# An 11th table looked up by one-hots, Gram blocks transposed straight out of PSUM, and tables loaded through embT

## The chip, the cores and the metric

The kernel runs on one core of a Trainium2 chip. The metric is the device time of one execution in microseconds (us). The program is written for each engine by hand: TensorE (PE; its weight loads appear as PEld), VectorE (DVE), ScalarE (ACT), GpSimd (POOL) and SyncE (SP) each run their own list of instructions in order, and meet only at semaphores.

## What is computed

2048 samples are scored by a recommender tower. Each sample has 27 ids, one for each of 27 tables with rows of 128 floats; tables have 1000, 1250, 12500 or 125000 rows.

```
e = stack([tbl_0[ids[:, 0]], ..., tbl_26[ids[:, 26]]], axis=1)   # 2048 x 27 x 128
dot = einsum('bnd,bmd->bnm', e, e)                              # 27 x 27 for each sample
z = the 351 entries of dot below its diagonal
h = concatenate([z, dense_ctx], axis=1)                         # 2048 x 367
h = maximum(h @ W_top1 + b_top1, 0)                             # 512
h = maximum(h @ W_top2 + b_top2, 0)                             # 256
y = h @ W_top3                                                  # 2048 x 1
```

## The kernel before

**Staging.** The samples go in 8 pairs `p` of 2 tiles `t` of 128 samples. Pair 0 and pair 7 are written out apart (`first`, `last`), pairs 1 to 6 are a hardware loop. The embeddings of a tile are wanted transposed, in `embT`, with the 128 numbers of a row on the partitions and 27 slots for each sample.

**Two ways to fetch a row.** Ten tables of 1000 rows stand in SBUF (`parts`, each split into a high and a low half so that two fp32r products give the fp32 value). A row is picked by a product with a one-hot matrix: DVE compares the ids with the row numbers (8 instructions for a table, four buffers `onehot`), PE does 16 matmuls for a table and 256 samples (`lookup`, L641), ACT copies two tables at a time to `embT`. The other 17 tables are gathered: POOL issues one indirect DMA for each tile and table (L376), 34 in a pair, into `rows`. `rows` has one buffer for each tile, so the gathers for pair p+1 start when PE has transposed the first group of tile t of pair p (`transpose_rows`, five groups `TR` of 4, 4, 4, 3 and 2 tables), and run beside what PE does next. POOL keeps one gather queued ahead of the one that runs (`one_queued`).

**A pair on PE** is: 160 lookup matmuls (with the first layer of the pair before between them), then for each tile 17 transposes, some calls of the MLP of the pair before, and `gram`: 128 products of 27 slots with themselves (L672; an fp32 matmul has two rows in the trace, so 256 rows for a tile), in two halves into two PSUM tiles. DVE copies the first half, ACT the second, to `blocks` (`keep_blocks`, L543 and L444); DVE then transposes 32 x 32 blocks of it to `turned` (`turn`, L551) and picks the 351 entries into `z`. After the second tile come the third layer, the transposes of `z` of tile 0, and the lookups of the next pair.

**Pair 0.** The ten tables come in through four staging buffers, in `turned`, `h1` and `blocks`, so a table's load waits until the one four places before it has been split: ACT makes the high half (L398), DVE the low one (L519). ACT makes two of pair 0's one-hots (`ACT_ONEHOTS`). Pair 0 looks up eight tables; the rows of tables 8 and 9 are gathered (`early_rows`, 4 indirect DMAs, L386) and transposed. A one-hot buffer is free when PE is done with its last table (`slot_free`). SP issues, in this order, tables, ids, weights, `dense_ctx`, and the ids of pair 1 that the gathers need (`load_idx`, L282).

```
STAGES = 4
TR = [range(0, 4), range(4, 8), range(8, 12), range(12, 15), range(15, 17)]
CALLS_AFTER = [{2: 2, 4: 4}, {2: 3, 4: 5}]
...
for k in range(STAGES, NM):
    sp.wait_ge(s_high, k - STAGES + 1)
    sp.wait_ge(s_low, k - STAGES + 1)
    load_table(k)
```

Of the kernel before, what the change touches and what calls it, by code (L numbers as in the profile page):

```python
# [44 lines left out]
GATHERED = [f for f in range(NF) if f not in MM_TABLES]  # L45
NG = len(GATHERED)
SLOTS = GATHERED + MM_TABLES
PARTS = 2

STAGES = 4  # L50
OH = 4

# [4 lines left out]
TR = [range(0, 4), range(4, 8), range(8, 12), range(12, 15), range(15, 17)]  # L57
NT = len(TR)

EARLY = range(NM - LOOK_TABLES, NM)  # L60
BUILT = NM - len(EARLY) - len(ACT_ONEHOTS)


JOBS = LOOK + TILES * NT
EMB_BANKS = 4
BANK = [k % EMB_BANKS for k in range(JOBS)]
BY_DVE = LOOK * [0] + TILES * [0, 1, 0, 1, 0]
DVE_JOBS = sum(BY_DVE)
ACT_JOBS = JOBS - DVE_JOBS

IDS = [range(0, 2), range(2, OH), range(OH, NM)]


CALLS_AFTER = [{2: 2, 4: 4}, {2: 3, 4: 5}]
# [6 lines left out]
def row_job(t, k):  # L81
    return LOOK + t * NT + k
# [4 lines left out]
GS = 16  # L87
STEPS = G // GS
# [28 lines left out]
def dlrm_tower(nc, ids, ids_mm, ident_in, dense_ctx, tables, W1, b1, W2, b2, W3, out):  # L117
    with ExitStack() as ctx:
# [9 lines left out]
        def sb_view(tile, first, dims, start=0, count=P):  # L128
# [6 lines left out]
        row_of = sb("row_of", [P, CH], F32)  # L135
        row_of_i = sb("row_of_i", [P, CH], I32)
# [5 lines left out]
        parts = sb("parts", [P, NM, PARTS, CH * D], F32R)  # L142

        idx = sb("idx", [P, TILES, NF], I32)
        rows = sb("rows", [P, TILES, NG, D], F32)
        early_rows = sb("early_rows", [P, TILES, len(EARLY), D], F32)
        ids_b = sb("ids_b", [P, NM, W], I32)
        onehot = sb("onehot", [P, OH, CH, W], F32R)
        embT = sb("embT", [P, TILES, P * SLOT + COLS - NF], F32)
        blocks = sb("blocks", [P, TILES, NJ, G], F32)  # L150
        turned = sb("turned", [P, TILES, JEXT * 32], F32)
# [3 lines left out]
        h2 = sb("h2", [P, N2, W], F32)  # L155

        y = sb_view(early_rows, 0, [[1, W]], 0, 1)
        y_last = sb_view(early_rows, W, [[1, W]], 0, 1)
# [10 lines left out]
        s_early = sem("s_early")  # L169
        s_w1 = sem("s_w1")  # L170
        s_stage = [sem(f"s_stage{k}") for k in range(STAGES)]
# [22 lines left out]
        gram_dve = sem("gram_dve")  # L194
        gram_act = sem("gram_act")
# [27 lines left out]
        def looked(p, k):  # L223

            if isinstance(p, int) and p == 0:
                return k + 1
            return p * LOOK + k

        def slot_free(eng, p, f):

            if f % LOOK_TABLES:
                eng.wait_ge(emb_filled, p * JOBS + f // LOOK_TABLES + 1)
            else:
                eng.wait_ge(s_looked, looked(p, f // LOOK_TABLES))

        def lookup_views(k):

            pitch = P * SLOT + COLS - NF
            return (sb_view(embT, NG + LOOK_TABLES * k, [[1, LOOK_TABLES], [pitch, TILES], [SLOT, P]]),
                    emb_ps[BANK[k]][:].rearrange("d (f t b) -> d f t b", f=LOOK_TABLES, t=TILES))  # L240

# [13 lines left out]
        def block_views(t, s):  # L255

            src = gram_ps[s][:, 0:GS * NJ].rearrange("p (g j) -> p g j", g=GS)
            return sb_view(blocks, t * NJ * G + GS * s, [[1, GS], [G, NJ]]), src

# [3 lines left out]
        def _(sp):  # L263
# [7 lines left out]
            def ids_read(p, h):  # L271

                done = max(OH, IDS[h].stop)
                if isinstance(p, int) and p == 0:
                    done = min(done, EARLY.start)
                    sp.wait_ge(onehot_act, sum(f < done for f in ACT_ONEHOTS))
                    sp.wait_ge(s_onehot, done - sum(f < done for f in ACT_ONEHOTS))
                else:
                    sp.wait_ge(s_onehot, BUILT + (p - 1) * NM + done)
# [4 lines left out]
            def load_table(k):  # L284
                src = tables[MM_TABLES[k]].rearrange("(p c) d -> p (c d)", c=CH)
                load_in_two(sp, stage[k % STAGES], src, s_stage[k % STAGES])
# [13 lines left out]
            load_ids(0, 2)  # L300
            sp.dma_start(ident[:], ident_in).then_inc(s_ident, 16)
# [535 lines left out]
```

## Time and profile before

| What | Value |
|---|---|
| Time, median of 3 runs | 703.17 us (702.69 to 704.76) |
| Time of the profiled execution | 701.53 us |
| Its span, first to last instruction | 699.7 us |
| Busy: PE, PEld, DVE, ACT, POOL | 392.1, 344.1, 257.3, 157.7, 263.0 us |
| Mean granted TensorE clock | 0.741 of full speed |
| DMA | 35.77 MB, 51 GB/s |

Busy time is the time in which an engine has an instruction running. No engine is busy for much over half of the span. PE waits for nothing that the profile can name in much of its idle time: such time is called "issue".

### The profile page before, as it was taken

How to read it: one execution, taken by the hardware profiler on the slowest of the kernel's cores; microseconds unless marked ns; L12 is line 12 of the kernel's file. 1: busy time of each engine (PE TensorE's matmuls, PEld its weight loads, DVE VectorE, ACT ScalarE, POOL GpSimd, SP SyncE). 2: the span in 40 equal slices, each digit the busy share in tenths (PEclk: the TensorE clock that was granted, in tenths of full speed). 3: DMA queues.
4: the chain of work that ended last, by engine and by line, in shares of the span. 5: the costliest groups of instructions: out<-in, count | busy, mean ns of one | idle time of the engine just before them, and what ended most of it. 6: DMA issues, size and time to landing. Idle time of an engine off the chain costs nothing.

```text
span 699.7 us, 15045 instructions
## 1 busy us (share of the span) xinstructions
PE 392.1 (56%) x6064; PEld 344.1 (49%) x6064; DVE 257.3 (37%) x733; ACT 157.7 (23%) x212; POOL 263.0 (38%) x281
## 2 busy tenths in 40 slices
PE   3216332595437926297154954289361982559875
PEld 3116231593326915197143944179151971439754
DVE  5305122482134714085041921257140850417121
ACT  2407210032111402033020322014020330203321
POOL 6770547106371074503562064701645035630000
PEclk9657656597567966599575986679675895759998
DMA  8924311111121121111111211211111121110000
GB/s 202 232 53 122 94 31 50 47 50 41 24 53 44 48 53 28 45 32 65 45 38 28 75 38 30 53 39 50 49 34 41 32 65 45 38 27 2 2 2 1
DMA packets 22699, 35.77 MB, mean 51 GB/s; under 512 B 12921, under 2 KB 13569, under 8 KB 22674
## 3 DMA queue, kind: packets, MB, share of 16 engines
q0 software_dynamic: 8832, 18.11, 10.2%
q1 hardware_dynamic: 13842, 17.32, 9.0%
q8 instruction: 18, 0.29, 0.2%
q14 instruction: 7, 0.06, 0.0%
HBM read 35.39 MB, written 0.01 MB: 51 GB/s over the span
## 4 chain that ended last, share of the span: by engine, by line
PE 51%; issue 37%; another core or an unknown queue 4%; ACT 4%; DVE 2%; DMA 2%; SPq 1%; DVEq 0%; ACTq 0%
PE emb_ps L641 19%; PE gram_ps L672 14%; PE mlp_ps L691 5%; PE emb_ps L664 5%; PE mlp_ps L705 4%; DMA turned<-in_tbl 2%; PE mlp_ps L734 1%; PE mlp_ps L713 1%; DVE onehot L531 1%; PE mlp_ps L682 1%; ACT parts L398 1%; ACT embT L415 1%; PE mlp_ps L739 1%; SPq L253 1%
## 5 line engine op out<-in xcount | busy, mean ns | idle before, releaser
L376 POOL DMA_INDIRECT rows<-in_tbl,idx x272 | 258.9, 952 | 354.4 <-PE emb_ps L664 239.7
L672 PE MATMUL gram_ps<-embT 128*32 128x26 f32 x4096 | 99.5, 222 | 248.2 <-issue 244.6
L672 PEld LDWEIGHTS gram_ps<-embT 128*32 128x32 f32 x4096 | 78.2, 143 | 272.6 <-issue 269.7
L641 PE MATMUL emb_ps<-onehot,parts 125*128 125x256 f32 x1248 | 165.9, 292 | 47.3 <-issue 43.2
L531 DVE TENSOR_SCALAR onehot<-ids_b,row_of 128x256 fp32r<-128x256 int32 x608 | 167.3, 355 | 50.3 <-remote 29.2
L641 PEld LDWEIGHTS emb_ps<-onehot,parts 125*128 125x128 f32 x1248 | 159.7, 198 | 50.2 <-issue 44.7
L543 DVE COPY blocks<-gram_ps 128x416 f32<-128x416 f32 x16 | 14.6, 910 | 293.6 <-PE gram_ps L672 293.6
L444 ACT ACTIVATE blocks<-gram_ps 128x416 f32<-128x416 f32 x16 | 14.2, 885 | 333.5 <-PE gram_ps L672 333.5
L415 ACT ACTIVATE embT<-emb_ps 128x512 f32<-128x512 f32 x40 | 48.1, 1224 | 102.5 <-PE emb_ps L641 102.5
L537 DVE COPY embT<-emb_ps 128x512 f32<-128x512 f32 (+1 forms) x32 | 33.3, 1046 | 58.3 <-PE emb_ps L664 54.4
L419 ACT ACTIVATE embT<-emb_ps 128x512 f32<-128x512 f32 (+1 forms) x48 | 45.8, 1067 | 10.0 <-PE emb_ps L664 7.0
L664 PE MATMUL emb_ps<-ident,rows 128*128 128x128 f32 x272 | 41.8, 300 | 0.9 <-ACT embT L419 0.5
L691 PE MATMUL mlp_ps<-zT,w_sb 128*128 128x256 f32 (+1 forms) x168 | 39.8, 379 | 0.0
L664 PEld LDWEIGHTS emb_ps<-ident,rows 128*128 128x128 f32 x272 | 34.8, 155 | 4.7 <-ACT embT L419 1.0
L691 PEld LDWEIGHTS mlp_ps<-zT,w_sb 128*128 128x128 f32 (+1 forms) x168 | 30.2, 189 | 3.5
L705 PE MATMUL mlp_ps<-h,w_sb 128*128 128x256 f32 x112 | 28.7, 404 | 0.0
L705 PEld LDWEIGHTS mlp_ps<-h,w_sb 128*128 128x128 f32 x112 | 22.1, 208 | 2.7
L430 ACT ACTIVATE h<-mlp_ps,b_sb 128x256 f32<-128x256 f32 x42 | 17.6, 470 | 25.7 <-PE mlp_ps L691 15.6
L551 DVE STREAM_TRANSPOSE turned<-blocks 128x832 f32<-128x832 f32 x16 | 16.6, 1040 | 15.2 <-ACT blocks L444 15.2
L407 ACT ACTIVATE onehot<-ids_b,row_of 128x256 fp32r<-128x256 int32 x16 | 6.6, 495 | 28.9 <-remote 28.9
L713 PE MATMUL mlp_ps<-h,w_sb 128*1 128x256 f32 x28 | 11.2, 543 | 1.8 <-ACT h L430 1.8
L566 DVE COPY z<-turned 128x351 f32<-128x351 f32 x16 | 9.4, 587 | 1.7
(37 smaller groups left out, 104.6 us busy)
## 6 DMA issues: line engine op xcount, KB each, us to landing
ids_b<-in_ids_mm SPq DMA_DIRECT2D x8, 768.0 KB
rows<-in_tbl,idx POOLq DMA_INDIRECT x272
ids_b<-in_ids_mm SPq DMA_DIRECT2D x16, 256.0 KB, 3.4
turned<-in_tbl SPq DMA_DIRECT2D x6, 448.0 KB
h<-in_tbl SPq DMA_DIRECT2D x2, 448.0 KB
blocks<-in_tbl SPq DMA_DIRECT2D x2, 448.0 KB
w_sb<-in_W_top SPq DMA_DIRECT2D x1, 512.0 KB, 6.8
w_sb<-in_W_top SPq DMA_DIRECT2D x2, 224.0 KB
```

Of the source, the lines that this page charges most:

```text
L376: pool.indirect_dma_start(rows[:, t, n, :], None, tables[f], bass.IndirectOffsetOnAxis(idx[:, t, f:f + 1], 0), engine_sem=gathers_written) ...
L415: nc.scalar.activation(*lookup_views(k), ACT.Copy).then_inc(emb_act, 1)
L419: nc.scalar.activation(*row_views(t, k), ACT.Copy).then_inc(emb_act, 1)
L430: last = nc.scalar.activation(dst[:, n, :], mlp_ps[job % 2][:, m * W:(m + 1) * W], ACT.Relu, bias=bias[:, n:n + 1])
L531: last = nc.vector.tensor_scalar(onehot[:, k % OH, c, :], ids_b[:, k, :], row_of[:, c:c + 1], None, ALU.is_equal)
L537: nc.vector.tensor_copy(*row_views(t, k)).then_inc(emb_dve, 1)
L641: last = nc.tensor.matmul(emb_ps[BANK[k]][:, m * W:(m + 1) * W], parts[0:MP, f, part, c * D:(c + 1) * D], onehot[0:MP, f % OH, c, :], star ...
L664: done = nc.tensor.transpose(bank[:, m * P:(m + 1) * P], rows[:, t, n, :], ident[:])
L672: last = nc.tensor.matmul(gram_ps[s][q * COLS:(q + 1) * COLS, g * NJ:(g + 1) * NJ], embT[:, t, at:at + COLS], embT[:, t, at:at + NJ], star ...
L691: done = nc.tensor.matmul(mlp_ps[job % 2][:, m * W:(m + 1) * W], w1_sb[0:K1[c], c, n * P:(n + 1) * P], zT[0:K1[c], c, :], start=(c == 0), ...
L705: done = nc.tensor.matmul(mlp_ps[0][:, m * W:(m + 1) * W], w2_sb[:, n, m * P:(m + 1) * P], h1[:, n, :], start=(n == 0), stop=(n == N1 - 1))
L713: done = nc.tensor.matmul(mlp_ps[1][0:1, 0:W], w3_sb[:, m:m + 1], h2[:, m, :], start=(m == 0), stop=(m == N2 - 1))
```

## The change

- **An 11th table.** The first table of 1250 rows (`X`) is looked up by one-hots from pair 1 on. It is split in 10 chunks of 125 rows, so it takes 20 more matmuls (`lookup_x`) and 10 more one-hot instructions a pair, in two halves of five chunks (`XHALVES`), each a tenant of the one-hot buffers; `NE` = 12 tenants instead of 10. It is split into halves on ACT and DVE during pair 0 (`split_x_high`, `split_x_low`). In pair 0 its rows are gathered (`x_rows`, 2 indirect DMAs) and transposed.
- **Gathers.** 16 tables are gathered, in four groups of four (`TR`): 32 indirect DMAs a pair. Pair 0 looks up all ten tables of 1000 rows, and has 34 gathers where it had 38.
- **Gram.** One PSUM tile over two banks with 32 columns for each block; `keep_blocks` and `blocks` are gone, and DVE transposes from PSUM to `turned` (`flip`), which has one buffer. `fill_z` is the rest of what `turn` did, issued later. The next `gram` waits for `flip`.
- **Staging.** Each table has a staging place of its own: six in `embT`, the others in `turned`, `h1`, `w1_sb` and `w2_sb`. SP issues all ten loads at once. The load of table X waits for the 7th low half, and the loads of the weights for the 10th. The first copy to `embT` waits for the 6th.
- **MLP calls** that stood between groups of transposes stand behind the last group (`CALLS_AFTER`).

```diff
-TR = [range(0, 4), range(4, 8), range(8, 12), range(12, 15), range(15, 17)]
+TR = [range(0, 4), range(4, 8), range(8, 12), range(12, 16)]
-CALLS_AFTER = [{2: 2, 4: 4}, {2: 3, 4: 5}]
+CALLS_AFTER = [{3: 6}, {3: 8}]
...
-        stage = [turned[:, t, 0:CH * D] for t in range(TILES)] + [
-            sb_view(h1, 0, [[1, CH * D]]), sb_view(blocks, 0, [[1, CH * D]])]
+        stage = [sb_view(embT, t * (P * SLOT + COLS - NF) + k * CH * D, [[1, CH * D]])
+                 for t in range(TILES) for k in range(EMB_STAGES // TILES)] + [
+            turned[:, 0:CH * D], sb_view(h1, 0, [[1, CH * D]]),
+            sb_view(w1_sb, 0, [[1, CH * D]]), sb_view(w2_sb, 0, [[1, CH * D]])]
+        x_stage = turned[:, 0:XCH * D]
...
-        gram_ps = [ps(f"gram_ps{k}", [P, 512]) for k in range(STEPS)]
+        gram_ps = ps("gram_ps", [P, G * COLS])
...
-            for k in range(STAGES, NM):
-                sp.wait_ge(s_high, k - STAGES + 1)
-                sp.wait_ge(s_low, k - STAGES + 1)
+            for k in range(5, NM):
                 load_table(k)
             for h in range(2):
                 ids_read(0, h)
                 load_ids(1, h)
+            sp.wait_ge(s_low, EMB_STAGES + 1)
+            load_in_two(sp, x_stage, tables[X].rearrange("(p c) d -> p (c d)", c=XCH), s_x_stage)
+            sp.wait_ge(s_low, NM)
...
-            def keep_blocks(p, t, s):
-
-                step = t * STEPS + s
-                dve.wait_ge(gram_filled, p * TILES * STEPS + step + 1)
-                nc.vector.tensor_copy(*block_views(t, s)).then_inc(gram_dve, 1)
+            def flip(p, t):
+
+                dve.wait_ge(gram_filled, p * TILES + t + 1)
+                past(dve, s_z, p * TILES + t)
+                nc.vector.transpose(turned[:, 0:NJ * G], gram_ps[:].rearrange("p (g j) -> p j g", g=G)[:, 0:NJ, :]
+                                    ).then_inc(s_turned, 1)
...
+            def lookup_x(p):
+
+                bank_free(p, XJOB)
+                pe.wait_ge(s_x_low, 1)
+                for h in range(XHALVES):
+                    pe.wait_ge(s_onehot, BUILT + (p - 1) * NE + NM + h + 1)
+                    for part in range(PARTS):
+                        for c in range(XH):
+                            at = (h * XH + c) * D
+                            last = nc.tensor.matmul(emb_ps[BANK[XJOB]][:, 0:W], x_parts[0:MP, part, at:at + D],
+                                                    onehot[0:MP, (NM + h) % OH, c, :],
...
-            def gram(p, t, s):
-                past(pe, (gram_dve, gram_act)[s], p * TILES + t)
-                for g in range(GS):
+            def gram(p, t):
+                past(pe, s_turned, p * TILES + t)
+                for g in range(G):
```

PE in the loop over pairs 1 to 6, from the last two of the ten lookups to the first Gram, before:

```order
33 L636 REGISTER_ALU
34 L641 MATMUL emb_ps<-onehot,parts 128x256 x16
35 L221 REGISTER_ALU
36 L662 ISA
37 L664 MATMUL emb_ps<-ident,rows 128x128 x4
38 L221 REGISTER_ALU
39 L664 MATMUL emb_ps<-ident,rows 128x128 x4
40 L221 REGISTER_ALU
41 L664 MATMUL emb_ps<-ident,rows 128x128 x4
42 L691 MATMUL mlp_ps<-zT,w_sb 128x256 x2
```

and at the same place of the change:

```order
39 L670 MATMUL emb_ps<-onehot,parts 128x256 x16
40 L232 REGISTER_ALU
41 L682 REGISTER_ALU
42 L686 MATMUL emb_ps<-onehot,x_parts 128x256 x10
43 L682 REGISTER_ALU
44 L686 MATMUL emb_ps<-onehot,x_parts 128x256 x10
45 L232 REGISTER_ALU
46 L704 ISA
47 L706 MATMUL emb_ps<-ident,rows 128x128 x4
```

The 20 matmuls of table X stand between the tenth lookup and the first group of transposes, which is the one that lets the next gathers start.

DVE in pair 0, from the one-hot of table 5 to the first copies to `embT`, before:

```order
11 L531 TENSOR_SCALAR onehot<-ids_b,row_of 128x256 x8
12 L519 TENSOR_TENSOR parts<-turned,parts 125x1024
13 L519 TENSOR_TENSOR parts<-h,parts 125x1024
14 L531 TENSOR_SCALAR onehot<-ids_b,row_of 128x256 x8
15 L519 TENSOR_TENSOR parts<-blocks,parts 125x1024
16 L519 TENSOR_TENSOR parts<-turned,parts 125x1024 x2
17 L537 COPY embT<-emb_ps 128x4x128
```

and in the change:

```order
10 L564 TENSOR_SCALAR onehot<-ids_b,row_of 128x256 x8
11 L542 TENSOR_TENSOR parts<-embT,parts 125x1024
12 L542 TENSOR_TENSOR parts<-turned,parts 125x1024
13 L564 TENSOR_SCALAR onehot<-ids_b,row_of 128x256 x8
14 L542 TENSOR_TENSOR parts<-h,parts 125x1024
15 L564 TENSOR_SCALAR onehot<-ids_b,row_of 128x256 x8
16 L542 TENSOR_TENSOR parts<-w_sb,parts 125x1024
17 L564 TENSOR_SCALAR onehot<-ids_b,row_of 128x256 x8
18 L542 TENSOR_TENSOR parts<-w_sb,parts 125x1024
19 L570 COPY embT<-emb_ps 128x4x128 x2
```

Two one-hots (of tables 8 and 9, 8 instructions each) are new, and the last two splits stand behind one of them each.

SP in pair 0, from pair 1's first ids to the ids for pair 1's gathers, in the change:

```order
26 L281 DMA ids_b<-in_ids_mm 128x512 x2
27 L271 DMA turned<-in_tbl 112x1280
28 L271 DMA turned<-in_tbl 13x1280
29 L271 DMA w_sb<-in_W_top 128x512
...
34 L326 DMA w_sb<-in_W_top 128x4x256
...
38 L345 DMA z<-in_dense_ctx 128x2x11
39 L345 DMA z<-in_dense_ctx 128x2x5
40 L294 DMA idx<-in_ids 128x27
```

Before, the two rows of table X are not there and the weights follow the two rows of `ids_b` without a wait; now a wait for the tenth low half stands ahead of the first `w_sb` row, and everything behind it, the `idx` of pair 1 too, comes after it.

## Rows read from the trace of the kernel before

**Rows 1.** The page's chain that ended last: shares of the span by engine.

```profile
PE 51%; issue 37%; another core or an unknown queue 4%; ACT 4%; DVE 2%; DMA 2%; SPq 1%; DVEq 0%; ACTq 0%
```

**Rows 2.** Timeline, POOL and PE around one tile's Gram, and the next tile's.

```profile
405.92 0.94 POOL L376 DMA_INDIRECT rows<-in_tbl,idx  x1 [31.80 <-PE emb_ps L664]
...
425.89 0.94 POOL L376 DMA_INDIRECT rows<-in_tbl,idx  x1 [0.30 <-issue]
430.05 1.17 PE L672 MATMUL gram_ps<-embT 128*32 128x26 f32 x70 [0.51 <-issue]
...
454.74 0.94 POOL L376 DMA_INDIRECT rows<-in_tbl,idx  x1 [0.30 <-issue]
458.88 2.98 PE L672 MATMUL gram_ps<-embT 128*32 128x26 f32 x204 [0.49 <-issue]
```

**Rows 3.** Gram matmuls by stretch: window, length, PE busy (count), PEld, clock, DMA, GB/s.

```profile
404.20:430.00 25.80, 4.10 (x55) 2.21 (x55) 0.67 0.17 43
430.00:433.00 3.00, 2.93 (x201) 2.82 (x201) 0.50 0.00 0
649.50:660.00 10.50, 2.80 (x256) 2.58 (x256) 0.94 0.02 3
```

**Rows 4.** Gather instructions by stretch: window, length, POOL busy (count), clock, DMA, GB/s.

```profile
404.20:430.00 25.80, 16.04 (x17) 0.67 0.17 43
627.80:700.00 72.20, 0.00 (x0) 0.90 0.01 2
```

**Rows 5.** Timeline of pair 0's gathers, first and last of 38, and behind them.

```profile
3.49 1.09 POOL L376 DMA_INDIRECT rows<-in_tbl,idx  x1 [2.51 <-issue]
...
50.60 0.95 POOL L376 DMA_INDIRECT rows<-in_tbl,idx  x1 [0.30 <-issue]
57.23 3.15 PE L641 MATMUL emb_ps<-onehot,parts 125*128 125x256 f32 x14 [0.34 <-issue]
57.33 2.19 DVE L531 TENSOR_SCALAR onehot<-ids_b,row_of 128x256 fp32r<-128x256 int32 x8 [29.20 <-remote]
```

**Rows 6.** Timeline of the lookups of one pair: PE and DVE.

```profile
386.49 7.82 PE L641 MATMUL emb_ps<-onehot,parts 125*128 125x256 f32 x64
394.14 2.76 PE L691 MATMUL mlp_ps<-zT,w_sb 128*128 128x256 f32 x12
384.54 12.71 DVE L531 TENSOR_SCALAR onehot<-ids_b,row_of 128x256 fp32r<-128x256 int32 x48 [0.69 <-PE emb_ps L641]
398.84 4.30 DVE L531 TENSOR_SCALAR onehot<-ids_b,row_of 128x256 fp32r<-128x256 int32 x16 [1.59 <-PE emb_ps L641]
```

**Rows 7.** Timeline of pair 0 behind its gathers: DVE, PE, SP, POOL.

```profile
67.04 1.22 DVE L519 TENSOR_TENSOR parts<-blocks,parts 125x1024 fp32r<-125x1024 f32 x1
74.46 0.58 PE L672 MATMUL gram_ps<-embT 128*32 128x26 f32 x45 [1.17 <-ACT embT L419]
62.46 2.03 SPq L253 DMA_DIRECT2D w_sb<-in_W_top  x5
70.39 0.85 SPq L282 DMA_DIRECT2D idx<-in_ids  x1
74.71 0.94 POOL L376 DMA_INDIRECT rows<-in_tbl,idx  x1 [23.16 <-issue]
```

**Rows 8.** Timeline at the turn from pair 0 to pair 1: PE and DVE.

```profile
128.66 2.62 PE L672 MATMUL gram_ps<-embT 128*32 128x26 f32 x177 [0.51 <-issue]
130.35 4.26 DVE L531 TENSOR_SCALAR onehot<-ids_b,row_of 128x256 fp32r<-128x256 int32 x16
141.12 7.82 PE L641 MATMUL emb_ps<-onehot,parts 125*128 125x256 f32 x64
```

**Rows 9.** Timeline behind the last Gram.

```profile
683.37 0.86 ACT L444 ACTIVATE blocks<-gram_ps 128x416 f32<-128x416 f32 x1 [4.64 <-PE gram_ps L672]
684.32 1.04 DVE L551 STREAM_TRANSPOSE turned<-blocks 128x832 f32<-128x832 f32 x1 [3.64 <-ACT blocks L444]
```

**Rows 10.** Group of DVE's copies of Gram blocks: busy, mean ns, idle before.

```profile
L543 DVE COPY blocks<-gram_ps 128x416 f32<-128x416 f32 x16 | 14.6, 910 | 293.6 <-PE gram_ps L672 293.6
```

More of the change, by code:

```diff
@@ L44 @@
 MM_TABLES = [f for f in range(NF) if SIZES[f] == MM_ROWS][:NM]
-GATHERED = [f for f in range(NF) if f not in MM_TABLES]
+XR, XCH, XHALVES = 1250, 10, 2
+XH = XCH // XHALVES
+X = SIZES.index(XR)
+IDS_TABLES = MM_TABLES + [X]
+GATHERED = [f for f in range(NF) if f not in IDS_TABLES]
 NG = len(GATHERED)
-SLOTS = GATHERED + MM_TABLES
+SLOTS = GATHERED + IDS_TABLES
 PARTS = 2
-STAGES = 4
 OH = 4
+EMB_STAGES = 6
+NE = NM + XHALVES
 ACT_ONEHOTS = (3, 6)
@@ L365, in body @@
             def body(p, first, last):
-                extra = 0 if first else TILES * len(EARLY)
+                extra = 0 if first else TILES
                 for t in range(TILES):
@@ L491, in body @@
                         if not BY_DVE[row_job(t, k)]:
[L492 removed]
+                            if last and t and k == NT - 2:
                                 layers(p - 1, 3)
@@ L502, in body @@
                         layers(p - 1, 2 + t)
-                    keep_blocks(p, t, 1)
+                    if first and t == 0:
+                        split_x_high()
                 if not last:
@@ L527, in make_onehot @@
                 elif not (isinstance(p, int) and p == 0):
[L528 to L532 removed]
+                    held = NM if isinstance(p, int) and p == 1 else NE
+                    slot_free(dve, p - 1, [e for e in range(held) if e % OH == k][-1])
+                of, first = (k, 0) if k < NM else (NM, CH + (k - NM) * XH)
+                for c in range(CH if k < NM else XH):
+                    last = nc.vector.tensor_scalar(onehot[:, k % OH, c, :], ids_b[:, of, :],
+                                                   row_of[:, first + c:first + c + 1], None, ALU.is_equal)
                 last.then_inc(s_onehot, 1)
@@ L581, in _ @@
             for k in range(OH, NM):
-                if k not in ACT_ONEHOTS and k not in EARLY:
+                if k not in ACT_ONEHOTS:
                     make_onehot(0, k)
@@ L586, in body @@
             def body(p, first, last):
-                for k in range(LOOK):
-                    if not first and OH + k * LOOK_TABLES < NM:
-                        for f in range(LOOK_TABLES):
-                            make_onehot(p, OH + k * LOOK_TABLES + f)
+                if not first:
+                    for k in range(OH, NE):
+                        make_onehot(p, k)
                 if not last and not first:
-                    make_onehot(p + 1, 2)
-                    make_onehot(p + 1, 3)
+                    make_onehot(p + 1, 0)
+                    make_onehot(p + 1, 1)
                 for t in range(TILES):
@@ L753, in lookups @@
                 for k in range(LOOK):
-                    if first and k == LOOK - 1:
-                        transpose_early()
-                    else:
-                        lookup(p, k)
+                    lookup(p, k)
                     if not first and k == 0:
@@ L796, in body @@
                     emb_moved(p, t)
-                    gram(p, t, 0)
-                    gram(p, t, 1)
-                if first:
-                    pe.wait_ge(s_low, NM)
-                elif not last:
+                    gram(p, t)
+                if not first and not last:
                     third_layer(p - 1)
```

196 lines of the change are left out of this document (103 added, 93 removed).

## The prediction, made blind

> **What bounds the kernel now.** I read the chain that ended last first: PE has 51% of it and "issue" 37% [rows 1]. So no engine's work is the bound; in over a third of the time PE waits for something that has no name. I looked for it by stretches. A Gram without gathers beside it is done in the 10.5 us window of the last pair with 2.80 us busy for its 256 matmul rows. In the loop the same 256 rows need from 404.2 to 433.0: 55 of them in 25.8 us, then 201 in 3.0 us [rows 3]. In that 25.8 us window POOL issues its 17 gathers; in the last pair there is none [rows 4]. The timeline shows both edges. The last gather of a tile starts at 425.89 and ends 0.94 later, at 426.83; PE wakes at 430.05, 3.2 us on. In the next tile the last gather ends at 455.68 and PE wakes at 458.88, again 3.2 us [rows 2]. Pair 0 repeats it with 38 gathers: the last ends at 51.55, PE wakes at 57.23, and DVE, which waits for PE to free a one-hot buffer, starts at 57.33 after 29 us of idleness [rows 5]. I conclude: while gathers are in flight PE hardly advances, and what it has queued is done when they end. The rows don't say why. The gathers come one every 1.25 us: 16 intervals between 405.92 and 425.89 are 19.97 us [rows 2].
>
> So a loop pair is the lookups on PE, plus twice (start of the gathers, 17 x 1.25 us, 3.2 us to wake, 3 us for the rest of the Gram). Other engines' work in the Gram windows lies under the gathers. A gather less is 1.25 us less; a lookup matmul stands between the windows and costs its full time.
>
> **Part 1, table X in the loop.** 64 lookup matmuls start at 386.49 and what follows them at 394.14, so one takes 7.65 / 64 = 0.12 us [rows 6]. 20 more are 2.4 us a pair, in pairs 1 to 7: +16.8 us. They stand ahead of the first group of transposes, which starts the gathers, so nothing hides them. DVE makes a one-hot instruction in 12.71 / 48 = 0.265 us [rows 6]: the first half of X (5, 1.3 us) waits, as the one-hots at 398.84 did, for table 6 and is done near 400.3; the second waits for table 7 and is done near 402; PE wants them at 404.2 and 405.4. Over 3 us of cover; without it DVE would add what it is late by, seven times. The two one-hots for the next pair that follow end near 406.7, when PE has just begun transposes, so DVE's copy is at most some tenths late, and it lies under the gathers. The extra ACT copy is half of one of 1.2 us, also beside PE.
>
> **Part 2, gathers.** 32 instead of 34 for each of pairs 1 to 7, and they run beside pairs 0 to 6. For the six loop pairs: 6 x 2 x 1.25 = -15.0 us. One transpose less for each tile lies beside the gathers, except in pair 7, where two are worth some tenths that I leave out. The MLP calls behind the last group are the same calls. Loop and pair 7 together: 16.8 - 15.0 = +1.8 us. **The 11th table alone brings nothing in the steady state.**
>
> **Part 3, pair 0.** Four gathers fewer, and at 48.06 / 38 = 1.265 us each (3.49 to 51.55 [rows 5]) PE wakes 5.0 us earlier, at 52.2. Behind that DVE is the chain. Before, the low half of table 7 ended at 68.26, 11.0 us after waking [rows 7]. Now a one-hot (2.19), a low half (1.22) and the same again stand behind it [rows 5, 7]: 6.8 us, so the tenth low half is at 52.2 + 11.0 + 6.8 = 70.0. SP then needs, as from 62.46 to 70.39, 7.9 us for weights and context until it issues pair 1's idx; the first gather comes 4.3 us behind that [rows 7]: 82.3, where it was 74.71. This is 7.6 us late, and it is paid, since the gathers of pair 1 are what PE waits for. But the first Gram starts at about 75.4 (74.46 before [rows 7]; behind the tenth low half at 70.0 come table 9's last 8 matmuls, 1.0, and on ACT the copies of two tables, of X and of two groups of rows, together some 4.4) and is over, some 4 to 6 us later, before any gather flies, and the second tile's gathers can follow the first's at once: 32 x 1.25 = 40.0 us without the gap. Before, PE woke at 128.66 [rows 8]; now at 82.3 + 40.0 - 0.3 + 3.2 = 125.2. **Net -3.5 us.**
>
> Before, PE then waited for two one-hots, ran its first lookups, and began the third at 141.1 [rows 8]. Now the first lookups need only one-hots that are ready, and the wait is at the transposes of z of tile 1: rest of the Gram 2.6, flip 1.0, two one-hots 4.3 [rows 8], the picking into z 1.3, transposes 0.3: 134.7. That is **-6.4 us** to the same point, 3.5 of it from above and 2.9 new.
>
> **Part 4, Gram from PSUM.** In the loop the ACT and DVE copies (0.9 us) lay beside PE, and so does flip; the next Gram starts 5.5 us after it, so even 2 us are covered. Without that cover it would be 1 to 2 us a tile. At the very end it is on the path. ACT's copy and the transpose took 683.37 to 685.36, 2.0 us [rows 9]. Flip is not in the trace: it costs at least what the transpose from SBUF took, 1.04 [rows 9], and at most twice DVE's copy of 416 elements out of PSUM, 1.82 [rows 10]. The end gains 0.2 to 0.95 us; I take 0.9, as for 832 elements the transpose is the nearer row. The last tile's rows now end in a copy of four tables after h2, where one of two stood: +0.5 us. Sum of the tail: -0.4.
> The Trainium skill ("VectorE: DVE Perf Modes", "Why PSUM operands drop a tier") says that an fp32 operand in PSUM holds DVE at one element a cycle. By it flip is an estimated 0.9 us and a fixed part, about the 1.04 of the row from SBUF, and the tail is as I took it; by the copy's row the tail is +0.3. No row of before shows a transpose out of PSUM.
>
> **Sum.** -6.4 + 1.8 - 0.4 = -5.0 us against the profiled execution's own 701.5 us: 696.5. The median of the runs is 1.6 us above that profile, so 703.2 - 5.0 = **698.2 us**.
>
> **Rivals.**
> - *Forecast*, 62%: pair 0 gains 3 to 9 us, the loop nothing. Its own range is 693 to 700.5.
> - *The gain of pair 0 is lost*, 17%: ten tables loaded at once make the gathers slower than 1.265 us each, or the wait of SP for the tenth low half costs more than 7.6 us. For it: no row shows gathers beside ten tables' loads at once. Against it: four tables came in beside the first gathers, and the 38 still kept 1.265 us on average [rows 5]. Each 1 us by which pair 1's gathers start later costs 1 us, until the -5.0 is gone: 701 to 705.
> - *PE's stall doesn't shrink with the gathers*, 16%, and the kernel is slower. Then the 20 matmuls a pair come on top: nothing comes back for the 12 x 1.25 and the 5.0 in pair 0, so -5.0 + 15.0 + 5.0 = +15: 718. For it: the rows show when PE wakes and not why, and two gathers out of 34 is a small step. Against it: 38 gathers held it to 57, 17 for 20 us, both ending 3 to 6 us behind the last. It decides from where a gather less returns under 1.25 x (1 - 5.0 / 20) = 0.94 us.
> - *More than forecast*, 5%: pair 1's idx come sooner, or the second Gram of pair 0 slips out ahead of the stall too (-2.6 more): 690 to 693.
>
> **The numbers.** About 0.3%, 2 us, can be told from no change here. Faster by more than that: 0.62 x 0.97 + 0.05 + a fifth of the second case, 0.68. Within it: most of the second case and the rest of the first, 0.14. Slower: 0.18. The range for 8 in 10 is 692 to 707: it leaves out the far part of the slow case and of the fast one.
>
> **What will show it.** Gathers every 1.25 us, 16 in a window; PE waking 3.2 us behind the last; a loop pair as long as before within 0.3 us, with lookups 2.4 us longer and each Gram window 1.25 shorter. In pair 0 PE wakes near 52, the idx of pair 1 is issued near 78, the first Gram runs without a stall, and PE wakes near 125. If the loop pair is longer by 1 us or more, the third case or DVE's cover is at fault; if pair 0 ends later than 128, the second.

## The result, and the profile after

The change makes the kernel slower: 708.22 us median of 4 runs (705.33 to 710.76) against 702.93 us (697.13 to 704.76), a ratio of 1.0105 (95% interval 1.0058 to 1.0152). I had forecast 698.2 us.

The page of the kernel after: its span, the DMA queue that brings instructions (packets, MB, share), the chain that ended last, and the group of the new transposes out of PSUM.

```profile
span 703.5 us, 15274 instructions
...
q8 instruction: 36, 0.59, 0.4%
...
PE 52%; issue 32%; another core or an unknown queue 7%; DVE 3%; DMA 2%; ACT 2%; SPq 1%; DVEq 0%; ACTq 0%
...
L576 DVE STREAM_TRANSPOSE turned<-gram_ps 128x832 f32<-128x832 f32 x16 | 16.8, 1050 | 309.4 <-PE gram_ps L714 284.8
```

The same queue on the page of the kernel before:

```profile
q8 instruction: 18, 0.29, 0.2%
```

"issue" fell from 37% [rows 1] to 32%, as fewer gathers should make it, yet the time rose. What has doubled is a queue that I had not looked at: 36 instruction packets instead of 18. The view of DMA queues, asked pass by pass of the loop, says when. In the passes that start at 211.1, 380.7 and 552 us it has no such line. For the windows 291.1 to 380.7 and 460.8 to 552 it has this one in each:

```profile
q8 instruction: 9, 0.15, 0.7%
...
q8 instruction: 9, 0.15, 0.8%
```

So every second pass of the loop, the third and the fifth, fetches code again. The queue's row names no engine; the packets start at 291.8 and 461.1 us, within 0.7 us of PE's jumps back at 291.1 and 460.8, so I took it for PE's code, and experiments 1 and 4 change nothing but PE's list of instructions. The timeline of after at the head of the pass that begins at 291.1, PE and DVE:

```profile
292.02 0.55 PE L724 MATMUL mlp_ps<-ident,z 128*128 128x128 f32 x3
...
296.13 3.13 PE L670 MATMUL emb_ps<-onehot,parts 125*128 125x256 f32 x13 [3.56 <-issue]
299.67 3.24 PE L670 MATMUL emb_ps<-onehot,parts 125*128 125x256 f32 x19 [0.41 <-issue]
300.51 2.19 DVE L564 TENSOR_SCALAR onehot<-ids_b,row_of 128x256 fp32r<-128x256 int32 x8 [7.14 <-PE emb_ps L670]
```

The first 32 lookups follow the transposes of z and should take some 4 us. Here PE stands still for 3.56 us with nothing to wait for, goes on in pieces and is done at 302.9. The first 13 lookups behind the standstill take 3.13 us, where 32 take 4.03 in a pass without a fetch (c_p48 of experiment 6). The granted clock says why (window, length, PE busy, clock, DMA, GB/s; the trace of after, then that of c_p48):

```profile
296.13:299.26 3.13, 3.13 (x13) 0.50 0.20 67
...
295.73:299.76 4.03, 4.03 (x37) 1.00 0.29 85
```

0.50 is the level of 1.2 GHz, 1.00 that of 2.4. The clock fell at 294.7, when PE had stood still since 292.6. So a fetch costs twice: some 4.0 us of standing still (3.56 + 0.41) and 2.3 us in which the 32 lookups run slower (6.37 us instead of 4.03). No gather flies here: the next begin at 324.8.

The sum by stretches, from first gather to first gather, after against before:

| Stretch | Before | After | Difference | Forecast |
|---|---|---|---|---|
| Start to the first gather of pair 2 | 160.55 | 156.62 | -3.9 | -4.0 |
| Five periods to that of pair 7 | 408.8 | 422.1 | +13.3 | -0.5 |
| From there to the end of the span | 130.3 | 124.7 | -5.6 | -0.5 |

(The forecast column splits my sum: -6.4 and one pair's 2.4 of table X; then 2.4 - 2.5 a pair; then 2.4 - 2.5 - 0.4.) The middle row alone overturns it. The periods of after are 81.3, 86.9, 82.7, 89.2 and 82.0 us, those of before 81.3 to 82.6.

What was forecast for single steps is there. Gathers and PE around one Gram, the timeline of after, which answers [rows 2], and the Gram's matmuls in its two windows, as in [rows 3]:

```profile
407.51 0.94 POOL L391 DMA_INDIRECT rows<-in_tbl,idx  x1 [34.22 <-PE emb_ps L706]
...
426.24 0.94 POOL L391 DMA_INDIRECT rows<-in_tbl,idx  x1 [0.30 <-issue]
...
430.19 2.90 PE L714 MATMUL gram_ps<-embT 128*32 128x26 f32 x197 [0.50 <-issue]
```

```profile
405.80:430.30 24.50, 4.16 (x66) 0.67 0.15 43
430.30:433.20 2.90, 2.79 (x197) 0.50 0.00 0
```

16 gathers in 18.73 + 0.94 us, and PE awake 3.0 us behind the last (forecast 3.2). Pair 0 and its end, the timeline of after, which answers [rows 5, 7, 8]:

```profile
51.83 4.75 PE L670 MATMUL emb_ps<-onehot,parts 125*128 125x256 f32 x23 [0.33 <-issue]
...
67.99 1.22 DVE L542 TENSOR_TENSOR parts<-w_sb,parts 125x1024 fp32r<-125x1024 f32 x1
...
74.61 0.43 SPq L294 DMA_DIRECT2D idx<-in_ids  x1
...
78.71 0.94 POOL L391 DMA_INDIRECT rows<-in_tbl,idx  x1 [31.09 <-issue]
...
102.42 0.95 POOL L391 DMA_INDIRECT rows<-in_tbl,idx  x1 [4.04 <-remote]
...
125.17 2.88 PE L714 MATMUL gram_ps<-embT 128*32 128x26 f32 x195 [0.51 <-issue]
...
134.83 7.82 PE L670 MATMUL emb_ps<-onehot,parts 125*128 125x256 f32 x64
```

Forecast were 52.2, 70.0 for the end of the last low half (69.2), 78 and 82.3 for idx and the first gather, 125.2 and 134.7. Two errors cancel here: the gathers of pair 1 start 3.6 us sooner than I said, but those of the second tile do not follow at once, they wait 4.04 us. Behind the last Gram, which answers [rows 9]:

```profile
687.82 1.05 DVE L576 STREAM_TRANSPOSE turned<-gram_ps 128x832 f32<-128x832 f32 x1 [4.78 <-PE gram_ps L714]
...
690.12 0.87 PE L772 MATMUL mlp_ps<-ident,z 128*128 128x128 f32 x3 [2.34 <-DVE z L591]
```

Flip takes 1.05 us. By the Trainium skill ("VectorE: DVE Perf Modes", "Why PSUM operands drop a tier") it was to be an estimated 0.9 us and a fixed part, by the copy's row up to 1.82: the trace agrees with the page.

### The profile page after: what moved, and what is told of

It reads as the page before. It is cut to its first block, busy times and chain, and to the rows that moved or that the text cites. A ratio compares the mean times of both kernels' runs of the same rounds, so it can differ in the third digit from the quotient of the medians.

```text
span 703.5 us, 15274 instructions
## 1 busy us (share of the span) xinstructions
PE 407.6 (58%) x6218; PEld 360.3 (51%) x6218; DVE 272.8 (39%) x804; ACT 142.0 (20%) x189; POOL 246.3 (35%) x264
## 4 chain that ended last, share of the span: by engine, by line
PE 52%; issue 32%; another core or an unknown queue 7%; DVE 3%; DMA 2%; ACT 2%; SPq 1%; DVEq 0%; ACTq 0%
PE emb_ps L670 20%; PE gram_ps L714 13%; PE mlp_ps L733 5%; PE emb_ps L706 4%; PE mlp_ps L747 3%; DMA embT<-in_tbl 2%; PE emb_ps L686 2%; DVE onehot L564 1%; PE mlp_ps L776 1%; PE mlp_ps L755 1%; PE mlp_ps L724 1%; SPq L271 1%; PE mlp_ps L781 1%; ACT onehot L425 0%
## 5 line engine op out<-in xcount | busy, mean ns | idle before, releaser
L391 POOL DMA_INDIRECT rows<-in_tbl,idx x256 | 244.0, 953 | 378.4 <-PE emb_ps L706 256.7
L564 DVE TENSOR_SCALAR onehot<-ids_b,row_of 128x256 fp32r<-128x256 int32 x694 | 193.5, 356 | 44.9 <-PE emb_ps L670 37.5
L670 PE MATMUL emb_ps<-onehot,parts 125*128 125x256 f32 x1280 | 176.1, 298 | 48.0 <-issue 31.5
L670 PEld LDWEIGHTS emb_ps<-onehot,parts 125*128 125x128 f32 x1280 | 168.4, 203 | 52.3 <-issue 48.4
L576 DVE STREAM_TRANSPOSE turned<-gram_ps 128x832 f32<-128x832 f32 x16 | 16.8, 1050 | 309.4 <-PE gram_ps L714 284.8
L436 ACT ACTIVATE embT<-emb_ps 128x512 f32<-128x512 f32 x40 | 48.9, 1232 | 118.9 <-PE emb_ps L670 118.9
L444 ACT ACTIVATE embT<-emb_ps 128x512 f32<-128x512 f32 x32 | 36.4, 1237 | 167.4 <-PE emb_ps L706 141.3
L570 DVE COPY embT<-emb_ps 128x512 f32<-128x512 f32 x32 | 35.4, 1185 | 28.4 <-PE emb_ps L706 28.4
L686 PE MATMUL emb_ps<-onehot,x_parts 125*128 125x256 f32 x140 | 17.7, 281 | 0.0
L686 PEld LDWEIGHTS emb_ps<-onehot,x_parts 125*128 125x128 f32 x140 | 17.0, 189 | 0.0
L448 ACT ACTIVATE zT<-mlp_ps 128x384 f32<-128x384 f32 x14 | 7.4, 528 | 25.7 <-PE mlp_ps L724 25.5
```

What stands on the lines that cost most here:

```text
L391: pool.indirect_dma_start(rows[:, t, n, :], None, tables[f], bass.IndirectOffsetOnAxis(idx[:, t, f:f + 1], 0), engine_sem=gathers_written) ...
L436: nc.scalar.activation(*lookup_views(k), ACT.Copy).then_inc(emb_act, 1)
L444: nc.scalar.activation(*row_views(t, k), ACT.Copy).then_inc(emb_act, 1)
L564: last = nc.vector.tensor_scalar(onehot[:, k % OH, c, :], ids_b[:, of, :], row_of[:, first + c:first + c + 1], None, ALU.is_equal)
L570: nc.vector.tensor_copy(*row_views(t, k)).then_inc(emb_dve, 1)
L670: last = nc.tensor.matmul(emb_ps[BANK[k]][:, m * W:(m + 1) * W], parts[0:MP, f, part, c * D:(c + 1) * D], onehot[0:MP, f % OH, c, :], star ...
```

## The experiments

A time given without a range is that of one profiled execution. Experiments that were run together shared one chip and are compared with the kernel before on it, whose time is given. Two kernels with one run each can't be told apart by less than some 1.5%, since the kernel before itself spreads over 11 us (688.93 to 699.92 on one chip).

**1. Move PE's loop, change nothing else.** Theory 1: the loop is refetched when it lies badly in the stream of PE's instructions. Idle waits at the start of PE's program, ahead of pair 0, move it.

```diff
+            for _ in range(200):            # 96, 48: two waits make one instruction
+                pe.wait_ge(s_pad, 1)
             sweep(pe, body)
```

> The changed kernel with 100 more instructions on PE ahead of its first work (waits for a semaphore that is long there; some 5 us in which PE has nothing to do anyway). Theory 1, instructions: every second pass of the loop over pairs PE's instructions are fetched anew (9 and 9 of the 16 KB packets of the instruction queue in the passes from 291 and 461 us), because the loop of about 1600 instructions lies over one block of 256 more than the old one of 1560 did; moved on by 100 it lies over one fewer, the fetches in the loop are gone, the pair periods of 86.9 and 89.2 us fall to 82, and the time falls by some 12 us, to 694 to 697. Theory 2, the loop is longer for another reason (waits of DVE, DMA traffic at the turn of the loop): nothing changes, 705 to 710.

> The same with 48 more instructions, loop start 1482. Theory 1: as with 24, and if the fetches are gone with 24 they are gone here too. Theory 2: 705 to 710.

> The same with 24 more instructions. Theory 1: the loop starts 1458 instructions in; whether the fetches are gone tells where the block's edge is (between 1434 and 1498 by the length of the loop); either 12 us less or nothing, no value between. Theory 2: as the changed kernel, 705 to 710.

Before on that chip: 700.5 us median. 100 instructions: **696.74 us** (median of 10, 694.32 to 699.11), ratio 0.9933 (0.990 to 0.9966), 19 packets on q8, none between those at 218.0 and 631.3 us. 48: 693.8 us in one run, 19 packets, none between those at 216.0 and 628.5 us. 24: **718.1 us** in one run, 36 packets, 9 of them in each of two passes. The same work is 24 us apart by 24 idle instructions. With its loop moved by 100, the change is faster than before.

The 718.1 is none of the values that I expected: the fetches stayed, and the time is some 10 us above the 708.2 of the change as it is. The trace shows a part of it. At the head of the third pass PE stands still twice, for 3.20 and 3.58 us, and the next 31 lookups take 6.00 us at a granted clock of 0.59. The same comes in the fifth pass, and the last stretch is 4.2 us longer than in after (128.9 for 124.7).

**2. One gathered table less in the kernel before.** It leaves out table 16 of the gathered ones (its slots are zero), so 16 gathers and transposes.

```diff
-GATHERED = [f for f in range(NF) if f not in MM_TABLES]
+ALL_GATHERED = [f for f in range(NF) if f not in MM_TABLES]
+GATHERED = ALL_GATHERED[:16]
...
```

> The kernel before with one gathered table left out (its slot is zeros; 16 gathers a tile, nothing put in its place). If a gather holds PE for 1.25 us: 16 fewer in all, of which 15 count (2 in pair 0's own row of gathers, 14 for pairs 1 to 7; the first two count too), so 20 us less, 682 to 684. If PE's stall has another length than the gathers' (the rival of the prediction): under 5 us less, 697 or more.

670.9 us in one run, -29.6 against 700.5, and below the 682 to 684 that I expected: 1.85 us a gather where I had 1.25. The five periods in the loop lost 13.6 us, 2.7 a pair, so 1.36 for a gather and its transpose: near my price. The rest is not all the gathers' price. In pair 0 the first `idx` of pair 1 was issued at 54.94 us and not at 70.39, and the first gather of pair 1 came at 68.64 instead of 74.71; b_p70 (experiment 3) has the same early `idx`, at 57.53, with all its gathers, and reaches the first gather of pair 2 4.4 us sooner than before (see 5). Behind pair 6 it lost 7.3 us. There the 24 matmuls of the first layer behind pair 7's first Gram took 2.94 us where the kernel before has 4.24, and the granted clock differs (the trace of before, then of b_16tables):

```profile
669.58:673.82 4.24, 4.24 (x25) 0.68 0.00 0
...
640.80:643.74 2.94, 2.94 (x24) 1.00 0.00 0
```

PE's stall does shrink with the gathers, by 2.7 us in a pair of the loop: the third rival falls.

**3. Move the loop of the kernel before.** If only the place decides, the old loop can be hit too. It has 1560 PE instructions, that of the change 1598 (records of a pass).

```diff
+            for _ in range(140):            # 176 in b_p88
+                pe.wait_ge(s_pad, 1)
             sweep(pe, body)
```

> The kernel before with 70 idle PE instructions ahead of the loop (140 waits on a semaphore that is long satisfied, two to an instruction). Theory 1, PE's loop is refetched in every second pass when it touches 8 blocks of 256 instructions instead of 7: the change was refetched with its loop at PE instructions 1434 to 3032 and 1458 to 3056, not with 1482 to 3080, so one block edge lies between 1458 and 1482 and the seventh one 1536 later. The loop before goes from 1379 to 2939; shifted by 70 to 1449..3009 it holds both edges if the first is at 1458 to 1473. Then 9 instruction fetches in each of two passes appear and the time is 700.5 + 10 to 13 = 710 to 714 us. If the edge is at 1473 to 1482, nothing changes here (700.5), and the next run, shifted by 88, must show it instead. Exactly one of the two, or both if the edge lies near 1470. Theory 2, the refetch belongs to something in the changed program (its longer loop, its other order), not to the place of the loop: no fetches and 700.5 in both.

> The kernel before with 88 idle PE instructions ahead of the loop: its loop stands at 1467 to 3027. Theory 1: it holds both edges if the first is at 1467 to 1482: 9 fetches in each of two passes and 710 to 714 us; otherwise as before. Theory 2: no fetches, 700.5 us.

Before on that chip: 694.3 us (688.93 to 699.92). Results 687.97 and 696.55 us, one run each, 18 packets each and no refetch of the loop. One packet of b_p88 lies inside the loop, at 299.0 us, behind its second jump back; the lookups there take 4.04 us, so it costs nothing that shows. My theory with edges exactly 1536 apart is refuted: they cannot lie where neither run hits them. Left were: the loop must also be long enough, or the refetch belongs to something else in the change.

**4. Lengthen the loop of the kernel before by 40 idle instructions.** It then has 1600, and none of the change's work.

```diff
             def body(p, first, last):
+                if not first and not last:
+                    for _ in range(80):
+                        pe.wait_ge(s_pad, 1)
                 lookups(p, first, last)
```

> The kernel before with 70 idle PE instructions ahead of the loop, as b_p70, and 40 more at the start of the loop: its loop has 1600 instructions and stands at 1449 to 3049, where that of b_p70 (no fetches in the loop) had 1560 at 1449 to 3009. The two runs b_p70 and b_p88 refuted theory 1 with an exact edge 1536 apart. Theory 1b: a refetch needs a start before a place between 1458 and 1482 and an end behind a place between 3027 and 3032, so that a loop of 1560 cannot or hardly be hit and one of 1600 can. Then this kernel, which has nothing of the change, shows 9 fetches in each of two passes, and against b_l40_p110 it is 10 to 13 us longer. Theory 2, the refetch needs something else of the changed program (its order, its waits): no fetches, no difference between the two.

> The kernel before with 110 idle PE instructions ahead of the loop and 40 at its start: 1600 instructions at 1489 to 3089. Both theories: no fetches in the loop beyond a single one. Its time is that of before and what 240 idle instructions in six passes cost, some us; it is the control of b_l40_p70.

**739.73 us** with the loop at 1449 to 3049, **724.15 us** at 1489 to 3089, beside 692.96 of one run of before; one run each. The second, which is the control, is itself 31 us above before, where I had expected some us: the idle instructions inside the loop are dear, and the comparison is between these two alone. The pages have:

```profile
span 737.9 us, 15361 instructions
...
q8 instruction: 36, 0.59, 0.3%
```

```profile
span 722.3 us, 15401 instructions
...
q8 instruction: 18, 0.29, 0.2%
```

The timeline of the first, and then of the second, at the head of the third pass:

```profile
307.18 0.90 PE L682 MATMUL mlp_ps<-ident,z 128*128 128x128 f32 x3
317.89 2.50 PE L641 MATMUL emb_ps<-onehot,parts 125*128 125x256 f32 x10 [9.80 <-issue]
```

```profile
308.40 0.88 PE L682 MATMUL mlp_ps<-ident,z 128*128 128x128 f32 x3
311.77 5.58 PE L641 MATMUL emb_ps<-onehot,parts 125*128 125x256 f32 x32 [2.49 <-issue]
```

The signature of the change, 9 packets in two of the passes and a standstill at their head, appears in a program that has nothing of the change except the length and place of its loop. b_p70 starts at the same 1449 with 1560 instructions and shows none: length and place are both needed. Against my expectation the price is 15.6 us, not 10 to 13: the two periods with a fetch are 8.0 us longer each, and the other three +4.1 in sum, and the start and the last stretch give 4.5 back.

The Trainium skill ("Runtime: NRT & Kernel Launch", "Instruction fetch mechanics") says that PE's instruction memory holds 2048 instructions and is refilled in order in blocks of 256, that a taken branch whose target is outside the current two-page window forces a fetch, and that the cost of a block's edge is mostly hidden. By the 2048 a loop of 1560 or of 1600 fits; by the two pages each pass would be fetched again. The traces agree with neither for all places: no packet at the jumps back of the kernel before (1560) and of b_l40_p110 (1600), 9 packets at every second one of b_l40_p70 (1600), whose two periods lose 8.0 us each.

**5. The other terms, on the change with 48 idle instructions.** First nearly all of table X's lookups left out (18 of 20 a pair, and with them most of its values):

```diff
-                    for part in range(PARTS):
-                        for c in range(XH):
+                    for part in range(1):
+                        for c in range(1):
...
```

> The change with 48 idle PE instructions ahead of the loop (693.8 us in one run), and of table X's 20 lookup matmuls a pair only 2 (one chunk and one part for each half): 18 x 7 matmuls are left out, and with them most of table X's values in the output. The one-hots and the gathers stay. Theory 1, a lookup matmul lies between the windows in which gathers hold PE and costs its full 0.12 us: -15.1 us, about 679. Rival: part of it lies under something else (DVE's one-hots for X or ACT's copies then end last): less than -10 us, over 684.

> The change with 48 idle PE instructions ahead of the loop, the same kernel as a_p48, timed in rounds against the one before. Theory 1: 0.990 to 0.993 of the time before, 693 to 696 us, since a_p48 gave 693.8 and a_p100 696.7. Rival: the single run was a lucky one and the gain is under 0.3%.

675.9 us in one run for a_x2, -16.6 against a_best's median of **692.43 us** (689.55 to 695.45); the five periods lost 2.55 us each where 18 x 0.12 = 2.2 was my price. A lookup costs its full time and a little more, 0.14 us. Before on this chip has a median of 694.3 us, and a_best against it is 0.9978 (0.9943 to 1.0013): short of the 0.990 to 0.993 that I expected, and not to be told from none.

Then flip done twice, and pair 1's `idx` ahead of the weights:

```diff
+                nc.vector.transpose(turned[:, 0:NJ * G], gram_ps[:].rearrange("p (g j) -> p j g", g=G)[:, 0:NJ, :]
+                                    ).then_inc(s_flip, 1)
+                dve.wait_ge(s_flip, p * TILES + t + 1)
                 nc.vector.transpose(turned[:, 0:NJ * G], gram_ps[:].rearrange("p (g j) -> p j g", g=G)[:, 0:NJ, :]
                                     ).then_inc(s_turned, 1)
```

```diff
+            for t in range(TILES):
+                for k in range(NT):
+                    sp.wait_ge(s_rows[t][k], 16 * len(TR[k]))
+                    sp.sem_inc(sp_waited, 1)
+                sp.wait_ge(s_x, 16 * TILES)
+                load_idx(1, t)
             sp.wait_ge(s_low, NM)
...
```

At their old place behind the weights the same loads are left out.

> The change with 48 idle PE instructions (692.4 us median in a_best, 693.8 in a_p48), and DVE transposes the Gram block out of PSUM twice, the second after the first is done: 16 more instructions of 1.05 us. My account (flip lies beside PE's stall or the lookups everywhere but behind the last Gram and where pair 0 turns into pair 1): +1 to +2.5 us. Rival (DVE's work behind a Gram is on the path in each pair, through the one-hots or the next Gram): up to 16 x 1.1 = +17 us.

> The change with 48 idle PE instructions, and pair 1's two idx loads issued ahead of the wait for the tenth low half and of the weights, not behind them. It undoes what I called 7.6 us late and paid. If each us by which pair 1's first gather starts earlier is a us gained, the gathers start when PE has transposed the first group of rows, near 75 where it was 79.4, and the time falls by 4 us. If instead the late start pays for itself, because the second tile's gathers cannot start before PE's transposes, which the first tile's gathers hold up, PE wakes about as before near 128 and the time is the same within 1.5 us.

Both came in below the kernel that they change: 686.45 and 686.21 us in one run each, beside 692.96 of one run of before. For a_flip2, where I expected 1 to 2.5 us more, this is no gain from a second flip. From the first gather of pair 2 to the end it takes 530.5 us, a_p48 531.9: the sixteen second flips are hidden. Between the first gathers of pairs 1 and 2 it takes 81.9 where a_p48 has 80.6: the +1.3 of my account. But pair 0 was 7.2 us shorter. The rows that differ are ACT's second one-hot, in a_flip2 and then in c_p48:

```profile
34.40 3.30 ACT L426 ACTIVATE onehot<-ids_b,row_of 128x256 fp32r<-128x256 int32 x8 [8.95 <-remote]
```

```profile
51.59 3.30 ACT L425 ACTIVATE onehot<-ids_b,row_of 128x256 fp32r<-128x256 int32 x8 [24.15 <-remote]
```

PE had started 85 lookup matmuls by 50 us there, and 58 in c_p48, before the gathers held it. Past some number the next one-hots are let go under the gathers instead of behind them. In the other 16 traces it was 48 to 74, and none has that one-hot early. The old program has an early case of its own: with 68 and 70 lookups started by 50 us, b_16tables and b_p70 issue the last loads of tables and the first `idx` under the gathers; with 49 to 58, before, b_p88 and the two of experiment 4 do so behind them. So pair 0 seems to vary by several us from run to run. No single program was traced in both cases, but a_p48, a_best and c_p48, which are one kernel, had 66, 58 and 58, and the kernel before spreads over 11 us on one chip. a_idx had an ordinary 58, so its gain was not of this kind, and experiment 6 times it again.

**6. Three kernels on one chip.**

> The same kernel as a_idx: the change with 48 idle PE instructions ahead of the loop and pair 1's idx loaded ahead of the weights. a_idx gave 686.2 beside 693.0 of one run of before, and pair 2's first gather at 154.17 where a_best had it at 160.24. Expected: 5 to 7 us below c_p48 of this call, 0.985 to 0.992 of before. Rival: the 6 us at pair 2 were the luck of one run (how far PE gets before the gathers of pair 0 hold it), and it is within 1.5 us of c_p48.

> The change with 48 idle PE instructions ahead of the loop, third time, for the comparison on one chip: 0.993 to 0.998 of before, as a_p100 and a_best.

> The change as it is, on the same chip as c_p48. Its loop is refetched in two passes. If that is all that separates them: 10 to 13 us above c_p48. If it is under 7 us, something else in the change also costs, and the two long periods are no full account.

Before on that chip: 695.16 us (690.37 to 701.12).

| Kernel | Median us | Ratio to before (95%) |
|---|---|---|
| c_after, the change | 706.22 | 1.0126 (1.0070 to 1.0182) |
| c_p48, its loop moved | 691.78 | 0.9946 (0.9918 to 0.9974) |
| c_idx, and `idx` early | **687.61** | 0.9893 (0.9854 to 0.9932) |

The place of the loop is worth 14.4 us, a little more than the 10 to 13 that I expected. POOL's first gather of each of the pairs 2 to 7, the timeline of c_after and then of c_p48:

```profile
156.62 0.94 POOL L391 DMA_INDIRECT rows<-in_tbl,idx  x1 [34.26 <-PE emb_ps L706]
240.14 0.94 POOL L391 DMA_INDIRECT rows<-in_tbl,idx  x1 [36.28 <-PE emb_ps L706]
327.21 0.94 POOL L391 DMA_INDIRECT rows<-in_tbl,idx  x1 [39.79 <-PE emb_ps L706]
411.36 0.94 POOL L391 DMA_INDIRECT rows<-in_tbl,idx  x1 [35.83 <-PE emb_ps L706]
497.82 0.94 POOL L391 DMA_INDIRECT rows<-in_tbl,idx  x1 [39.41 <-PE emb_ps L706]
581.20 0.94 POOL L391 DMA_INDIRECT rows<-in_tbl,idx  x1 [34.70 <-PE emb_ps L706]
```

```profile
159.17 0.94 POOL L391 DMA_INDIRECT rows<-in_tbl,idx  x1 [36.05 <-PE emb_ps L706]
241.78 0.94 POOL L391 DMA_INDIRECT rows<-in_tbl,idx  x1 [35.36 <-PE emb_ps L706]
321.63 0.94 POOL L391 DMA_INDIRECT rows<-in_tbl,idx  x1 [32.91 <-PE emb_ps L706]
403.25 0.94 POOL L391 DMA_INDIRECT rows<-in_tbl,idx  x1 [33.28 <-PE emb_ps L706]
484.49 0.94 POOL L391 DMA_INDIRECT rows<-in_tbl,idx  x1 [34.03 <-PE emb_ps L706]
563.93 0.94 POOL L391 DMA_INDIRECT rows<-in_tbl,idx  x1 [31.25 <-PE emb_ps L706]
```

The periods of c_after are 83.5, 87.1, 84.1, 86.5, 83.4, those of c_p48 82.6, 79.9, 81.6, 81.2, 79.4. The two periods with a refetch (the second and fourth) lose 7.2 and 5.2 us; the other three 7.4 us together; the start (-2.5) and the last stretch (-3.7) give 6.2 back. That is 13.6, the difference of the spans. b_l40_p70 against b_l40_p110 shows the same shape: +20.1 in the five periods, -3.4 behind them. So the lesser losses in the other passes seem to belong to the place of the loop as well. How they arise I have seen in one place only: in c_after a Gram stops for 1.12 us ahead of 382.47 and the first lookups behind it take 4.55 us at a granted clock of 0.87, in c_p48 there is no stop and they take 4.03 at 1.00.

The last stretch differs by short stops and the clock. In c_p48 the first Gram of pair 7 stops for 2.32 us ahead of 652.2, and the 16 matmuls of the second layer behind it take 5.30 us; in c_after two stops of 0.8 and 0.7 us stand around there, and the same matmuls are done in 4.47 us with the second of them (window, length, PE busy, clock, DMA, GB/s; c_p48, then c_after):

```profile
652.98:658.28 5.30, 5.30 (x20) 0.68 0.00 0
...
668.27:672.74 4.47, 3.77 (x20) 1.00 0.00 0
```

That the place of the loop decides this is not shown: a_p24, which is refetched too, has a last stretch of 128.9 us, c_after 123.2, c_p48 126.9.

c_idx is 4.2 us below c_p48, short of the 5 to 7 that I expected, and clear of the 1.5 of my rival. Its first gather of pair 1 starts at 71.85 instead of 78.41 and that of pair 2 at 154.43 instead of 159.17: of 6.6 us earlier 4.7 remain.

## Why the prediction was wrong

- **What bounds the kernel: right.** PE hardly moves while gathers fly, wakes 3 us behind the last, and follows their number (experiment 2).
- **Part 1 and Part 2, the terms: right in kind.** By experiment 5, where 18 lookups are worth 2.55 us, 20 cost 2.8 us a pair and not 2.4. 16 gathers follow each other at 1.25 us, and by experiment 2 one is worth 1.36 with its transpose. Both terms are short, and they offset each other.
- **The sum "Loop and pair 7 together: 16.8 - 15.0 = +1.8 us": the step that failed.** It prices PE's added instructions by their durations alone. It puts the place of the loop in the instruction stream at nothing, without a reason. The loop became 38 instructions longer and began 55 later (1434 instead of 1379), and with that it is fetched again in every second pass. The five periods from pair 2 to pair 7 cost +13.3 us in the profiled run where this sum had -0.5 for them. The place is worth +14.4 us on one chip (6), shown by moving the loop without touching its work (1), and in the old program too (4).
- **Part 3, pair 0: right to 0.1 us at the end, by errors that cancel** (above). "The second tile's gathers can follow the first's at once" is wrong in the profiled run: 4.04 us between them. With the loop moved, the same point, where the lookups of pair 1's third table start, lies at 137.4 in c_p48, 2.7 us later than forecast, behind a stop of 1.57 us in the Gram: so the 0.1 is luck in this too. "This is 7.6 us late, and it is paid": undoing it brings 4.2 us.
- **Part 4, flip: right**, 1.05 us for 1.04, hidden in the loop and on the path only at the turn and at the end. The last stretch came out 5.1 us shorter than forecast. That is not this part's merit: the traces of the same work range from 123.2 to 128.9 us by stops of PE and its granted clock (6), which the sum took at nothing.
- **The rivals.** None was this one. "If the loop pair is longer by 1 us or more, the third case or DVE's cover is at fault" names two culprits, and with a pair 2.7 us longer in the mean it was neither. The third named the right side of the result, and its reason, a stall that doesn't shrink, was false.
- **Without the refetch the sum was near:** 0.9946 of before is -3.8 us (-1.8 to -5.7), for -5.0 forecast; the other chips gave -0.7% and -0.2%. Its parts are not where I put them. Up to the first gather of pair 2 the trace of the moved kernel c_p48 gains 1.4 us on that of before where I had 4.0, in the five periods 4.1 where I had 0.5, and in the last stretch 3.5 where I had 0.5; a_p100, moved too, loses 2.6 in the periods (411.4 for 408.8). That the sum is near is in part luck.

Open: which rule sets the place. A refetch came with starts and ends of the loop at 1434 to 3032, 1458 to 3056 and 1449 to 3049; none with 1379 to 2939, 1449 to 3009, 1467 to 3027, 1482 to 3044, 1482 to 3080, 1489 to 3089 and 1534 to 3132. Ends up to 3027 and starts from 1482 on were safe; why, and why every second pass, the traces don't say.

## What to carry to other kernels

When a change makes a hardware loop longer or puts instructions ahead of it, count the loop's instructions per engine, and look at the DMA queue of instructions pass by pass: packets inside the loop mean that it is being fetched again. If they are there, some tens of idle instructions ahead of the loop are a cheap trial; here 48 were worth 14.4 us, more than everything the change had to give, while 24 left the fetches where they were. And where a stall holds an engine for most of the time, a gain found by moving loads (`idx` ahead of the weights, -4.2 us) can be larger than one from moving work between engines.

## What the runs showed of the hardware

- PE's loop of 1560 to 1600 instructions is kept over its passes in most places that were tried: no packet for 400 us, or a single one (b_p88, a_x2). In a bad place 9 packets come in every second pass, and PE stands still for 3.6 us at its head (after), or 9.8 us where the kept loop with the same 40 idle instructions has 2.5 (experiment 4).
- Behind such a standstill the granted clock was 0.50, and 13 lookups took 3.13 us where 32 take 4.03 at 1.00. The same 24 matmuls took 4.24 us at 0.68 and 2.94 at 1.00 (experiment 2).
- Between 24 and 48 idle PE instructions ahead of the loop lie 24 us (718.1 and 693.8, one run each).
- An idle instruction inside the loop, two waits that are long satisfied, is not free: with 40 a pass the last four periods are 85.4 us against 81.6, so 0.1 us each.
- VectorE's transpose of 832 fp32 values a partition takes 1.05 us out of PSUM and took 1.04 out of SBUF.
- How many matmuls PE gets done before the first gathers hold it differs from trace to trace, from 48 to 85 at 50 us; in the one with 85 pair 1's first gather came 7.2 us sooner.
